# ScalarE copies the transposed probabilities out of PSUM ahead of a unit's exponentials instead of behind them

## What is computed

```python
def _attention(x, Wq, Wk, Wv, Wo):
    q = (x @ Wq.T).reshape(b, s, H, HD)
    ...
    scores = jnp.einsum('bqhd,bkhd->bhqk', q, k) / np.sqrt(HD).astype(np.float32)
    scores = jnp.where(causal, scores, jnp.finfo(scores.dtype).min)
    probs = jax.nn.softmax(scores, axis=-1)
    out = jnp.einsum('bhqk,bkhd->bqhd', probs, v).reshape(b, s, d)
    return out @ Wo.T
...
attn = _attention(x, Wq, Wk, Wv, Wo)
mod = MOD_SCALE * jnp.tanh(attn @ A)
```

## Time and profile before

| | us |
|---|---|
| median of 3 runs | 1198.85 |
| the three runs | 1198.36, 1198.85, 1205.85 |
| the profiled execution, whole run | 1203.19 |
| its span, first to last instruction | 1201.4 |
| PE busy | 1020.9 (85%) |
| DVE busy | 686.8 (57%) |
| POOL busy | 485.8 (40%) |
| ACT busy | 363.4 (30%) |

### The profile page before, as it was taken

How to read it: one execution, slowest core, us unless ns; L and a number is a source line. 1 busy time by engine, 2 the same in 40 slices (tenths; PEclk the granted TensorE clock), 3 DMA queues, 4 the chain that set the end, 5 groups by cost and what they waited for, 6 DMA issues and landing times. The chain is left out here.

```text
span 1201.4 us, 23669 instructions
## 1 busy us (share of the span) xinstructions
PE 1020.9 (85%) x6301; PEld 840.8 (70%) x6301; DVE 686.8 (57%) x2250; ACT 363.4 (30%) x1114; POOL 485.8 (40%) x626
## 2 busy tenths in 40 slices
PE   5466898988998998988988879449999999999966
PEld 4354686776776876867767657338898888888855
DVE  2733456675665676666766555444555555555546
ACT  1024435344244254254254251001111111111233
POOL 0413214146155164163172260434565555555522
PEclk8777999999999999999999899779999999999989
DMA  9149950230311410410410410139999999999776
GB/s 360 67 105 288 288 125 1 61 73 33 89 49 36 105 36 27 105 40 23 105 41 14 114 39 8 54 111 293 304 320 302 307 296 293 296 286 311 243 282 219
DMA packets 129986, 184.67 MB, mean 154 GB/s; under 512 B 29749, under 2 KB 99989, under 8 KB 127517
## 3 DMA queue, kind: packets, MB, share of 16 engines
q1 hardware_dynamic: 94720, 104.41, 32.1%
q10 hardware_dynamic: 22989, 45.98, 11.1%
q0 software_dynamic: 12240, 33.83, 7.9%
HBM read 123.09 MB, written 61.60 MB: 154 GB/s over the span
## 5 line engine op out<-in xcount | busy, mean ns | idle before, releaser
L537 POOL TENSOR_TENSOR prob<-prob,rec 128x512 f32<-128x512 f32 x96 | 100.6, 1048 | 135.9 <-DVE rec L1309 134.5
L599 POOL DMA_INDIRECT y_rows<-sh_gu,ids x133 | 131.3, 987 | 59.9 <-POOL spare L290 56.6
L1020 ACT ACTIVATE prob<-bank,nmx 128x128 f32<-128x128 f32 (+1 forms) x256 | 105.0, 421 | 149.7 <-DVE nmx L1303 149.6
L1092 ACT ACTIVATE inv<-bank 88x256 f32<-88x256 f32 x159 | 60.4, 380 | 273.9 <-PE bank L930 272.1
L1525 DVE COPY sh_gu<-bank 128x256 f32<-128x256 f32 x133 | 56.5, 425 | 102.8 <-PE bank L939 102.8
L939 PE MATMUL bank<-w_in,inv 88*128 88x256 f32 x428 | 109.8, 379 | 0.0
L1303 DVE TENSOR_REDUCE nmx<-bank 128x2 f32<-128x512 f32 (+1 forms) x96 | 65.9, 686 | 75.4 <-PE bank L744 73.9
L562 POOL DMA_INDIRECT x_rows<-x_copy,desti x84 | 87.1, 1037 | 15.6 <-issue 15.6
L631 PE MATMUL bank<-cst,prob 128*128 128x128 f32 x384 | 59.8, 279 | 26.6 <-ACT probT L1027 26.6
L939 PEld LDWEIGHTS bank<-w_in,inv 88*128 88x128 f32 x428 | 72.8, 190 | 6.0
L631 PEld LDWEIGHTS bank<-cst,prob 128*128 128x128 f32 x384 | 45.0, 143 | 36.1 <-POOL prob L537 30.4
(11 more groups left out here) (264 smaller groups left out, 2289.7 us busy)
## 6 DMA issues: line engine op xcount, KB each, us to landing
w_in<-in_e_w ACTq DMA_DIRECT2D x107, 176.0 KB
w_down<-in_e_w SPq DMA_DIRECT2D x105, 176.0 KB
x_rows<-sgt SPq DMA_DIRECT2D x2, 8192.0 KB, 36.7
fwd<-x_rows SPq DMA_DIRECT2D x78, 132.0 KB
w_up<-in_e_w SPq DMA_DIRECT2D x54, 176.0 KB
w_up<-in_e_w ACTq DMA_DIRECT2D x52, 176.0 KB
w_down<-x_rows SPq DMA_DIRECT2D x54, 132.0 KB
stack_q<-q_parts SPq DMA_DIRECT2D x16, 384.0 KB, 5.9
```

The source lines that it names most:

```text
L537: pool.tensor_tensor(p, p, r, ALU.mult).then_inc(S["b_scaled"], 1)
L599: pool.indirect_dma_start(y_rows, bass.IndirectOffsetOnAxis(ap=ids[s][:].bitcast(U32), axis=0), yc[s], None).then_inc(S[f"m_st{s}"], 16)
L1020: i = act.activation(prob[:, u % PROBS, h * w:(h + 1) * w], psum(u % 2, h * w, (h + 1) * w), ACT.Exp, bias=nmx[:, u, h:h + 1], accum_out=s ...
L1092: act.activation(hs[n], bank[0:IH, 3 + n, 0:2 * P].rearrange("p (a b) -> p a b", a=2), ACT.Silu).then_inc(S["m_hs"], 1)
```

## The change

In ACT's part of a unit the copy of the turned probabilities of unit u - 3 now stands ahead of the exponentials of unit u. Operations, shapes, buffers and semaphore counts are the same.

```diff
             def unit(u):
                 def part(b):
+                    turned = u - BEHIND
+                    if 0 <= turned < UNITS:
+                        need(act, "b_pT", b * UNITS + turned + 1)
+                        need(act, "b_pv", b * PVS + pvs_of(turned - PROBTS))
+                        act.activation(probT[:, turned % PROBTS, :, :], bank[:, 2, :].rearrange("p (j q) -> p j q", j=4), ACT.Copy
+                                       ).then_inc(S["b_pT_out"], 1)
                     if u < UNITS:
                         act.wait_ge(S["b_max"], b * UNITS + u + 1)
                         need(act, "b_pT", b * UNITS + u - PROBS + 1)
...
                         i.then_inc(S["b_exp"], 1)
-                    turned = u - BEHIND
-                    if 0 <= turned < UNITS:
-                        need(act, "b_pT", b * UNITS + turned + 1)
-                        need(act, "b_pv", b * PVS + pvs_of(turned - PROBTS))
-                        act.activation(probT[:, turned % PROBTS, :, :], bank[:, 2, :].rearrange("p (j q) -> p j q", j=4), ACT.Copy
-                                       ).then_inc(S["b_pT_out"], 1)
                 return part
```

## The result

| | before | after |
|---|---|---|
| median, us (17 runs each) | 1200.61 | 1191.73 |
| lowest and highest run | 1198.19, 1211.40 | 1182.93, 1196.85 |
| ratio after / before, 95% interval | | 0.9907 (0.9881 to 0.9933) |
| the profiled execution, whole run | 1203.19 | 1187.16 |
| its span | 1201.4 | 1185.2 |

The kernel became faster, by 0.93% by the ratio and by 8.9 us (0.74%) between the medians. The forecast was 1184.6 us, 1.2% less than before, with a range from 1176 to 1195, which holds the 1191.73.

A forecast was written before the change was run, and what follows sets the result against it. PE was taken to stand idle in transposes behind ACT's copy, itself queued behind exponentials. Terms 3.8 + 4.5 + 2.4 + 1.4 + 2.1 = 14.2 us, taken from the median 1198.85, gave 1184.6 us; range 1176 to 1195.

The forecast's parts named there:

- POOL's scaling: Rival: the transposes wait for POOL's scaled probabilities, not for the copy, so the change does nothing: 1199 us, chance 0.08.
- The wait in u11: Transpose's stop of 1.69 us in six blocks goes; ACT's chain behind DVE's `nlg` leaves 0.64 of each: 3.8 us.
- The wait in u4: Transpose's stops in six blocks, 0.46, 0.92 and 4 x 0.78 us, go whole: 4.5 us.
- The product for d_wo: DVE's `vh`, behind the stop in u4: there at 356.15, PE arrives at 356.16, so nothing is lost.
- SECOND: Turn with fewer matmuls between units: 2.4 us saved in u6, 1.4 at the end's alternation, nothing for three waits between.
- no other queue changes: Claim about the whole change: 72 copies pass their unit's exponentials, they issue no transfer, and other engines' queues stay the same.
- LAST_BUT_ONE, 2.1: Turn with five waits, 4.2 us: those of u4 and u5 go nearly whole, 0.67 in u12 goes: 2.1 us.
- the stop of u7: Wait in LAST_BUT_ONE, followed by the x3 transposes, which wait for a DVE chain begun earlier: nothing saved.
- The cost, nothing: Exponentials start 0.25 us late in u6, elsewhere up to 0.4; one `scores` in SECOND might wait 0.3: taken as nothing.
- two or three as the limit of harmless: Sign of being wrong: `scores` (L741) waiting for exponentials more than two or three times in the profile after.
- More than the sum, by the clock: Rival: without stops, two slow-clock episodes may go, about 1.5 us each, and more 1.69 stops: 1177 us, chance 0.12.
- faster by over 1%: Chance 0.60 that the measurement shows this: 0.48 of the forecast case's 0.56, with the rival "more".

The follow-up runs named there:

- e8: The kernel before, with each copy done twice, one behind the other: 1232.33 us, ratio to before 1.0203.
- e6: The kernel after, with tile S1 set ahead of the router's part D4m in the turns' list: 1184.87 us, ratio to before 0.9838.
- e3: The kernel after, with the copy ahead only in the part of unit 10, elsewhere behind the exponentials: ratio to before 0.9965.
- e2: The kernel after, with the copy ahead only in the part of unit 3, elsewhere behind the exponentials: ratio to before 0.9969.
- e1: The kernel after, measured again without edit: 1196.87 us beside 1204.85 for the kernel before, ratio 0.9931.
- e10: The kernel after, with the copy ahead only in SECOND and the first blank fill of x_rows issued early on SP: 1202.26 us, one run.
- e9: The kernel after, with the copy ahead only in the turn SECOND, elsewhere behind the exponentials: 1199.87 us, one run.
- e11: The kernel before, with only the first blank fill of x_rows issued early on SP: 1202.21 us, ratio to before 0.9991.

## Why the prediction was right, and where it was not

**What bounds, and who releases the transpose.** Right. The copy was the releaser, not POOL's scaling: the waits under both names fell together (26.6 to 3.7 us, 30.4 to 3.5), and e8 moves them by the copy alone.

**The wait in u11, 0.64 a block.** Right, with its reason. The stop of 1.69 went, S2's wait rose from 0.95 to 2.05, so 0.6 remained (predicted 0.64), and e6 gives the other 1.1 back by taking `ex` out of the way. e3's 0.75 bears the bound out as well, though not by the longer wait of S2 that was expected there.

**The wait in u4, six blocks.** Right. e2 saves 0.69 against 0.78. The product for d_wo, with a margin of 0.01 us by the working, swallowed at most the 0.09 between them.

**SECOND.** The term was near (3.5 measured, 3.8 said), in part by luck: the granted clock moves this turn by up to 3 us in kernels with the same order (87.3 and 90.5 above). And the step behind it was left out. The sum treated the turn as if its end could come earlier at no price, and said "no other queue changes": true of the order, not of what the queue does in time. SP's chain of fills and `uT`, 76 us long, was by 0.6 us the next thing to end (its data came at about 168.5, the scores at 169.08 in the kernel before: issue 157.47, with the 11.06 us from issue to scores that after shows). SECOND and turn 2 together saved 87.29 + 83.01 - 83.79 - 84.48 = 2.03 us, where the sum had 3.8 + 1.1 = 4.9. This is the greatest miss, and the trace of before held the rows that show it.

**LAST_BUT_ONE, 2.1.** Too large. Turn 7 and the last block together saved 2.75; 1.59 of it is turn 7, so about 1.2 is left for LAST_BUT_ONE. The reading "the stops of u4 and u5 go nearly whole" didn't look at what follows a little later, the x3 transposes, which wait for a DVE chain:

```profile
694.08 1.12 PE L631 MATMUL bank<-cst,x_row 128*128 128x128 f32 x4 [3.86 <-DVE x_row L1165]
```

In the kernel before this wait was 2.02 us:

```profile
703.12 0.83 PE L631 MATMUL bank<-cst,x_row 128*128 128x128 f32 x4 [2.02 <-DVE x_row L1165]
```

The prediction used this wait against the stop of u7 and not against those of u4 and u5, though it takes back most of what comes ahead of it: it grew by 1.84, against 0.40 + 1.20 + 1.19 (u7's stop) that went. Part of the rest is clock: these four transposes took 1.12 us, those before 0.83.

**The cost, nothing.** Right. `scores` waited for exponentials 4 times, 3.7 us, instead of once; the three new ones are in SECOND (0.20, 0.55 and 1.06), inside the stretch that DVE's work ends (DVE is busy for 6.58 of the 7 us from 117 to 124). The prediction had named 0.3 there and two or three as the limit of harmless; four were harmless too, since the count says less than the place. In steady blocks there is none.

**More than the sum, by the clock.** This rival was priced as a gain, and it is a scatter. In the kernel before, turn 3 took 87.08 instead of 85.33 behind a stop of 1.69. After, that episode is gone, but turn 6 took 84.89 instead of 83.74, behind the longer stop of S2. Windows of ten us from the kernel after, first in turn 5, then at the same place of turn 6 (columns as in the earlier trace rows), and the row where it begins:

```profile
458.26:468.26 10.00, 7.60 (x65) 5.61 (x64) 5.57 (x24) 3.24 (x9) 4.33 (x5) 1.00 0.11 41
```

```profile
542.00:552.00 10.00, 7.95 (x47) 5.65 (x45) 4.63 (x22) 2.86 (x8) 4.32 (x5) 0.83 0.11 41
```

```profile
544.35 2.51 PE L865 MATMUL bank<-x3T,sh_gu 128*96 128x256 f32 x8 [2.05 <-DVE sact L1424]
```

The eight matmuls that took 1.97 us at 2.4 GHz (granted clock 1.00) took 2.51 here, where the window's mean of 0.83 shows part of it at 1.2 GHz; one turn lost 1.15 us. In e1 the same place, one turn of two that were disturbed:

```profile
377.78 3.65 PE L865 MATMUL bank<-x3T,sh_gu 128*96 128x256 f32 x8 [2.05 <-DVE sact L1424]
```

Of turns 2 to 6, 1 is such a turn in before's profile, 1 in after's, 2 in e1's, at other turns each time; none in e10's. Without them the profile pair gives 11.76 - 1.75 + 1.15 = 11.2 us, against the 14.2 of the sum; the medians give 8.9 and 8.0. The remaining 2 to 3 us could be more such episodes in the kernel after: 3 of its 10 stops of S2 (1.66 to 2.07 us) in the turns 2 to 6 of the two profiles were followed by one, none of before's stops of 0.95 there. But e6, with stops of 0.95 at that place, has two episodes elsewhere, and e2, with the stops of 1.69 as before, has three. Nor is the start of the kernel settled: turn 1 began 2.5 and 1.9 us later in the two profiles of the kernel after than in the one of before, in code that the change doesn't touch. The profiles are too few, and it stays open.

**The sizes.** Sum 14.2: SECOND and its follower 2.9 too much, LAST_BUT_ONE and turn 7 together 0.8 too much, the four turns between 0.6 too little: 11.1. The share of "faster by over 1%" was set at 0.60, on a sum that lay just 2 us above that bound; two missed followers of 1 to 3 us were enough to end on its other side.

## What to carry to other kernels

On an in-order engine, put the operation that empties a single PSUM bank ahead of operations that wait for something later, and measure the slack there by doubling it: 0.39 us a block ahead against 3.7 behind (1.5 of it waiting, the rest the clock that fell behind the longer stop) told more than any list of waits. For each stretch that becomes shorter ask which chain of another queue ends just behind it at its own pace, SP's transfers first: a gain in one turn was lost in the next by a transfer issued behind 60 us of fills. A wait that already ends a stretch can take back savings well ahead of it, not only the one next to it.

## What the runs showed of the hardware

In turns 2 to 6 of all profiles the clock fell to 1.2 GHz behind stops of TensorE of 1.61 us (e6, turn 6) to 4.45 us (e6, turn 2), once behind two stops of 0.78 and 1.08 us (e3, turn 6), in some turns and not in others that read alike. In before, after and e1 it cost 1.15 to 1.75 us each time. Behind the stop of 1.69 us in u11 it fell in 6 of 25 such turns (before, e2, e9, e10, e11), behind the 2.3 us that e8 has there in 5 of 5. I had taken such an episode for a property of its place.

`nlg`, an operation on 128x2 numbers, took 1.21 us in steady blocks of before and after and 0.17 us in e6. In the first case it started at 373.85, POOL's scaling ran from 373.97 to 375.02, and `nlg` ended at 375.06; in e6 POOL was issuing an indirect transfer. The Trainium skill, SBUF — State Buffer, section Who interferes with whom, says that VectorE's `tensor_scalar` can take the pair of ports that it shares with GpSimd, and that the one who issues second then stands still for the other's whole instruction. The trace agrees that one stood until the other was through, and it was DVE. But by the start times DVE came first, by 0.12 us, so which one stands isn't explained by these rows, and no run here changed the ports alone.
